# Attention heads with the values' high and low halves and ones in one stationary side of 96 columns

## What is computed

```python
def _L0_ffn_ref(x, Wq, Wk, Wv, Wo, w_ln1, w_ln2, Wr, Wg, Wu, Wd):
    xn = _rmsnorm(x, w_ln1)
    q, k, v = ...                      # 16 heads of 32 features
    attn = einsum('bqhd,bkhd->bhqk', q, k) / sqrt(32)
    attn = softmax(where(causal, attn, -inf))
    h = einsum('bhqk,bkhd->bqhd', attn, v)
    x = x + h @ Wo.T
    return x + moe(_rmsnorm(x, w_ln2))  # 8 experts, the best 2 per token
```

## Time and profile before

| | us |
|---|---|
| three executions | 1804.84, 1806.59, 1807.99 |
| median | 1806.59 |
| the profiled execution, its own time | 1806.42 |
| its span, first to last instruction | 1804.7 |
| TensorE busy | 1674.0 (93%) |
| its weight loads | 1422.9 (79%) |
| VectorE busy | 1106.8 (61%) |
| ScalarE busy | 981.3 (54%) |
| GpSimd busy | 510.0 (28%) |

### The profile page before, as it was taken

One profiled execution on the slowest core, in us unless ns is written; L12 is line 12 of the kernel. 1 busy time (PEld: TensorE's weight loads), 2 busy tenths in 40 slices (PEclk: granted clock), 3 DMA queues, 4 the chain that ended last, 5 costly groups with the idle time before them and its releaser, 6 DMA issues.

```text
span 1804.7 us, 26788 instructions
## 1 busy us (share of the span) xinstructions
PE 1674.0 (93%) x9270; PEld 1422.9 (79%) x9270; DVE 1106.8 (61%) x2076; ACT 981.3 (54%) x1713; POOL 510.0 (28%) x648
## 2 busy tenths in 40 slices
PE   3978899999989999999989999999999999999996
PEld 3666688877777777878777778898989898989895
DVE  6887732247776666676644745666666666665652
ACT  6465553335666655656553224565656656565652
POOL 3254220101212111313112022343434334343432
PEclk9989999999999999999999999999999999999998
DMA  6365558897687554875447556676767676767771
GB/s 233 94 187 185 184 168 248 231 280 256 196 266 193 174 166 114 241 199 160 147 143 181 193 199 210 227 245 231 243 227 251 228 258 225 255 226 246 233 237 24
DMA packets 119222, 370.17 MB, mean 205 GB/s; under 512 B 30175, under 2 KB 30175, under 8 KB 105378
## 3 DMA queue, kind: packets, MB, share of 16 engines
q1 hardware_dynamic: 98850, 329.36, 54.0%
q0 software_dynamic: 15696, 31.21, 9.5%
q10 hardware_dynamic: 4592, 8.52, 1.3%
HBM read 289.47 MB, written 85.72 MB: 208 GB/s over the span
## 4 chain that ended last, share of the span: by engine, by line
PE 61%; DVE 6%; ACT 5%; issue 3%; DMA 2%; SPq 1%; POOL 1%; ACTq 0%; DVEq 0%; POOLq 0%
PE bank L53 17%; PE bank L54 17%; PE bank L55 17%; PE bank L2290 2%; PE bank L2321 1%; PE bank L2318 1%; DVE hd_a L2072 1%; PE bank L2320 1%; PE bank L2276 1%; PE bank L2835 1%; ACT hd_relu L1919 1%; DVE ex_w_lo L2732 1%; DVE hd_p_lo L2139 1%; DVE hd_masked L2132 1%; ACT hd_a_hi L1940 1%
## 5 line engine op out<-in xcount | busy, mean ns | idle before, releaser
L2732 DVE TENSOR_TENSOR ex_w_lo<-ex_stage,ex_w_hi 128x1024 fp32r<-128x1024 f32 x207 | 248.7, 1237 | 166.9 <-ACT ex_w_hi L2642 162.3
L1841 POOL TENSOR_SCALAR_AFFINE_SELECT hd_p_full<-hd_p_full 128x128 f32<-128x128 f32 (+1 forms) x192 | 90.3, 478 | 433.2 <-ACT hd_p_full L1970 431.2
L2568 POOL TENSOR_TENSOR ex_a_lo<-ex_a,ex_a_hi 128x256 fp32r<-128x256 f32 x128 | 92.4, 745 | 288.4 <-ACT ex_a_hi L2664 288.2
L53 PE MATMUL bank<-ex_x_hi_a,ex_w_hi 128*128 128x256 f32 x512 | 145.0, 283 | 0.5 <-issue 0.5
L53 PE MATMUL bank<-ex_x_hi_b,ex_w_hi 128*128 128x256 f32 x512 | 144.7, 283 | 0.0
L55 PE MATMUL bank<-ex_x_hi_b,ex_w_lo 128*128 128x256 f32 x512 | 144.2, 282 | 0.0
L54 PE MATMUL bank<-ex_x_lo_b,ex_w_hi 128*128 128x256 f32 x512 | 144.2, 282 | 0.0
L55 PE MATMUL bank<-ex_x_hi_a,ex_w_lo 128*128 128x256 f32 x512 | 144.2, 282 | 0.0
L54 PE MATMUL bank<-ex_x_lo_a,ex_w_hi 128*128 128x256 f32 x512 | 144.0, 281 | 0.0
L2639 ACT ACTIVATE ex_w_hi<-ex_stage 128x1024 fp32r<-128x1024 f32 x134 | 133.7, 1048 | 0.1
L1970 ACT ACTIVATE hd_p_full<-bank 128x512 f32<-128x512 f32 (+1 forms) x192 | 93.3, 520 | 65.9 <-PE bank L2290 56.4
(11 more groups left out here) (318 smaller groups left out, 4884.6 us busy)
## 6 DMA issues: line engine op xcount, KB each, us to landing
ex_stage<-in_w_moe SPq DMA_DIRECT2D x69, 1536.0 KB, 7.7
first_w<-in_w_moe SPq DMA_DIRECT2D x23, 1536.0 KB, 6.8
hd_up<-scratch_up_halves SPq DMA_DIRECT2D x48, 512.0 KB, 6.4
hd_down<-scratch_down_halves SPq DMA_DIRECT2D x48, 512.0 KB, 6.0
st_qk<-scratch_qk SPq DMA_DIRECT2D x64, 256.0 KB, 4.2
st_qk<-scratch_qk SPq DMA_DIRECT2D x128, 64.0 KB, 3.7
scratch_up_halves<-hd_up SPq DMA_DIRECT2D x16, 512.0 KB, 3.3
scratch_down_halves<-hd_down SPq DMA_DIRECT2D x16, 512.0 KB, 3.8
```

The source lines that it names most:

```text
L53: pe.matmul(out, lhsT=w_hi, rhs=x_hi, start=first, stop=False)
L1841: pool.affine_select(out=p_full[:, i % 2, at:at + blocks * P], in_=p_full[:, i % 2, at:at + blocks * P], compare_op=ALU.is_ge, fill=0.0, b ...
L2568: pool.tensor_tensor(a_lo[:, chunk.par, m, :], a[:, m, :], a_hi[:, chunk.par, m, :].bitcast(F32), ALU.subtract).then_inc(wide_lo_ready, 1)
L2732: return dve.tensor_tensor(dst, src, hi.bitcast(F32), ALU.subtract)
```

## The change

The stationary side of a key block becomes one tile of 96 columns per head: 32 columns of high values, 32 of low values, 32 ones (`v_sides`; `v_hi`, `v_lo` and `v_one` are views of it). One matmul with `p_hi` and one with `p_lo` per key block go through it, so a head takes eight matmuls instead of twelve, and the bank then holds, for one head alone, 32 rows of high products, 32 rows of low products and 32 rows of denominators. (The product of the low halves is now part of the sum.)

Each head opens the bank anew. ScalarE copies the low rows to `o_sum` and takes Ln of the denominators after every head (`log_sums`); VectorE adds the bank's high rows to `o_sum` after every head (`add_halves`); Exp and the multiplication remain one per pair, the latter from `o_sum`. TensorE waits, ahead of a head, until both engines are through with the head before it. The split of the values takes one instruction per engine and pair instead of two. The zero fills are gone. In the diff:

```diff
--- before.py
+++ after.py
@@ -1439,8 +1439,7 @@
     STEPS = N + LAG + 2
     FIRST_PROJ = HEADS + LAG + 1
 
-    V_HI_COLS, V_HI_STEP, V_HI_TILE = 7 * HD, 4 * HD, 3 * HD
-    V_LO_COLS, V_LO_STEP, V_LO_TILE = 3 * HD, 2 * HD, HD
+    V_ROWS = 3 * HD
 
     S_PARTS = (((3, 0),), ((2, 0), (0, 3 * P)), ((1, 0),))
     T_PARTS = (((0, 0),), ((3, 0), (1, P)), ((2, 0),))
@@ -1565,8 +1564,10 @@
             hits = route.hits(lent)
         buffers.lend(buffers.OVER_VALUES)
         v_raw = sb("v_raw", [P, 2, TT, PAIR])
-        v_hi = sb("v_hi", [P, V_SLOTS, TT, V_HI_COLS], F32R)
-        v_lo = sb("v_lo", [P, V_SLOTS, TT, V_LO_COLS], F32R)
+        v_sides = sb("v_sides", [P, V_SLOTS, TT, 2, V_ROWS], F32R)
+        v_hi, v_lo, v_one = (v_sides[:, :, :, :, n * HD:(n + 1) * HD] for n in range(3))
+        o_sum = sb("o_sum", [PAIR, S])
+        sb("spare", [P, 2 * S])
         with ExitStack() as same:
             p_full, o, relu, a = (same.enter_context(nc.sbuf_tensor("hd_" + n, shape, F32)) for n, shape in (
                 ("p_full", [P, 2, PT_COLS]), ("o", [P, O_SLOTS, S]), ("relu", [P, DEEP, S]), ("a", [P, DEEP, S])))
@@ -1629,6 +1630,9 @@
         p_hi_ready = sem("p_hi_ready")
         p_lo_ready = sem("p_lo_ready")
         heads_done = sem("heads_done")
+        small_taken = sem("small_taken")
+        halves_added = sem("halves_added")
+        logs_ready = sem("logs_ready")
         rec_ready = sem("rec_ready")
         o_ready = sem("o_ready")
         o_hi_ready = sem("o_hi_ready")
@@ -1665,7 +1669,7 @@
         first_w_in = sem("first_w_in")
         first_rows = sem("first_rows")
 
-        CONSTS = 6
+        CONSTS = 3
         S_BANK, T_BANK = psum[0:2], psum[2:4]
         o_bank, misc_bank = psum[4], psum[7]
 
@@ -1806,12 +1810,9 @@
 
         @block.gpsimd
         def _(pool):
-            pool.memset(v_hi[:, :, :, :].bitcast(F32), 0.0).then_inc(consts_ready, 1)
-            pool.memset(v_lo[:, :, :, :].bitcast(F32), 0.0).then_inc(consts_ready, 1)
-            pool.wait_ge(consts_ready, 2)
-            for place in range(2):
-                at = 2 * HD + place * V_HI_STEP
-                pool.memset(v_hi[:, :, :, at:at + HD].bitcast(F32), 1.0).then_inc(consts_ready, 1)
+            for n in range(V_SLOTS):
+                i = pool.memset(v_one[:, n].bitcast(F32), 1.0)
+            i.then_inc(consts_ready, 1)
             pool.iota(prefer[:, :], [[-1, E]], base=E, channel_multiplier=0,
                       allow_small_or_imprecise_dtypes=True).then_inc(consts_ready, 1)
             pool.memset(minus_half[:, :], -0.5).then_inc(consts_ready, 1)
@@ -1974,23 +1975,25 @@
                 act.wait_ge(cut_ready, 3 * i + 3)
                 act.activation(p_hi[:, i % 2, :], p_full[:, i % 2, :], ACT.Copy).then_inc(p_hi_ready, 1)
 
+            def log_sums(h):
+                p, place = divmod(h, 2)
+                act.wait_ge(heads_done, h + 1)
+                if p and place == 0:
+                    act.wait_ge(o_ready, p)
+                own = slice(place * HD, (place + 1) * HD)
+                act.activation(o_sum[own, :], o_bank[HD:2 * HD, :], ACT.Copy).then_inc(small_taken, 1)
+                act.activation(sums_rec[own, :], o_bank[2 * HD:3 * HD, :], ACT.Ln).then_inc(logs_ready, 1)
+
             def inverse_sums(p):
-                act.wait_ge(heads_done, 2 * p + 2)
-                if p:
-                    act.wait_ge(o_ready, p)
-                act.activation(sums_rec[:, :], o_bank[PAIR:2 * PAIR, :], ACT.Ln).then_inc(rec_ready, 1)
-                act.wait_ge(rec_ready, 2 * p + 1)
+                act.wait_ge(logs_ready, 2 * p + 2)
                 act.activation(sums_rec[:, :], sums_rec[:, :], ACT.Exp, scale=-1.0).then_inc(rec_ready, 1)
 
             def high_v(p):
-                if p == 0:
-                    act.wait_ge(consts_ready, CONSTS)
                 act.wait_ge(v_in[p % 2], p // 2 * 16 + 16)
                 if p >= V_SLOTS:
                     act.wait_ge(heads_done, 2 * (p - V_SLOTS) + 2)
-                for place in range(2):
-                    act.activation(v_hi[:, p % V_SLOTS, :, place * V_HI_STEP:place * V_HI_STEP + HD],
-                                   v_raw[:, p % 2, :, place * HD:(place + 1) * HD], ACT.Copy).then_inc(v_hi_ready, 1)
+                act.activation(v_hi[:, p % V_SLOTS], v_raw[:, p % 2].rearrange("p t (u n) -> p t u n", n=HD),
+                               ACT.Copy).then_inc(v_hi_ready, 1)
 
             def high_o(p):
                 b, half, c = pair_cols(p)
@@ -2022,8 +2025,10 @@
                 for k in ks[:1]:
                     begin(k)
                     finish(k)
-                if 1 <= i <= N and i % 2 == 0:
-                    inverse_sums(i // 2 - 1)
+                if 1 <= i <= N:
+                    log_sums(i - 1)
+                    if i % 2 == 0:
+                        inverse_sums(i // 2 - 1)
                 if 0 <= i < N:
                     exps(i, 2)
                     high_p(i)
@@ -2139,14 +2144,20 @@
                 dve.tensor_tensor(p_lo[:, i % 2, :], p_full[:, i % 2, :], p_hi[:, i % 2, :].bitcast(F32),
                                   ALU.subtract).then_inc(p_lo_ready, 1)
 
+            def add_halves(h):
+                own = slice(h % 2 * HD, (h % 2 + 1) * HD)
+                dve.wait_ge(small_taken, h + 1)
+                dve.tensor_tensor(o_sum[own, :], o_bank[0:HD, :], o_sum[own, :], ALU.add).then_inc(halves_added, 1)
+
             def output(p):
                 b, half, c = pair_cols(p)
                 q = b * HC + c
                 own = slice(half * PAIR, (half + 1) * PAIR)
-                dve.wait_ge(rec_ready, 2 * p + 2)
+                dve.wait_ge(halves_added, 2 * p + 2)
+                dve.wait_ge(rec_ready, p + 1)
                 if half == 0 and q >= O_SLOTS:
                     dve.wait_ge(sum_done, sums_before[proj_at[(q - O_SLOTS) // HC]] + TT)
-                dve.tensor_tensor(o[own, q % O_SLOTS, :], o_bank[0:PAIR, :], sums_rec[:, :],
+                dve.tensor_tensor(o[own, q % O_SLOTS, :], o_sum[:, :], sums_rec[:, :],
                                   ALU.mult).then_inc(o_ready, 1)
 
             def low_o(p):
@@ -2157,13 +2168,9 @@
                                   o_hi[:, q % O_SLOTS, :].bitcast(F32), ALU.subtract).then_inc(o_lo_ready, 1)
 
             def low_v(p):
-                dve.wait_ge(v_hi_ready, 2 * p + 2)
-                for place in range(2):
-                    i = dve.tensor_tensor(v_lo[:, p % V_SLOTS, :, place * V_LO_STEP:place * V_LO_STEP + HD],
-                                          v_raw[:, p % 2, :, place * HD:(place + 1) * HD],
-                                          v_hi[:, p % V_SLOTS, :, place * V_HI_STEP:place * V_HI_STEP + HD].bitcast(F32),
-                                          ALU.subtract)
-                i.then_inc(v_lo_ready, 1)
+                dve.wait_ge(v_hi_ready, p + 1)
+                dve.tensor_tensor(v_lo[:, p % V_SLOTS], v_raw[:, p % 2].rearrange("p t (u n) -> p t u n", n=HD),
+                                  v_hi[:, p % V_SLOTS].bitcast(F32), ALU.subtract).then_inc(v_lo_ready, 1)
 
             def per_tile(x):
                 return x.unsqueeze(2).to_broadcast([P, TT, E])
@@ -2224,6 +2231,8 @@
                     finish(k)
                 if s < N:
                     maxima(s, 2)
+                if 1 <= i <= N:
+                    add_halves(i - 1)
                 if s % 2 == 1 and 0 <= (s - 7) // 2 < N // 2:
                     output((s - 7) // 2)
                 for k in ks[1:]:
@@ -2308,18 +2317,15 @@
                     pe.wait_ge(a_full, ups_before[TWO_UPS])
                 if place == 0:
                     pe.wait_ge(v_lo_ready, p + 1)
-                    if p:
-                        pe.wait_ge(o_ready, p)
+                if h:
+                    pe.wait_ge(logs_ready, h)
+                    pe.wait_ge(halves_added, h)
                 for kt in range(TT):
                     at = slice(T_AT[kt], T_AT[kt] + (TT - kt) * P)
-                    queries = slice(kt * P, S)
-                    high = v_hi[:, p % V_SLOTS, kt, place * V_HI_TILE:place * V_HI_TILE + 2 * PAIR]
-                    low = v_lo[:, p % V_SLOTS, kt, place * V_LO_TILE:place * V_LO_TILE + PAIR]
-                    pe.matmul(o_bank[:, queries], lhsT=high, rhs=p_hi[:, h % 2, at], start=(place == 0 and kt == 0),
-                              stop=False)
-                    pe.matmul(o_bank[0:PAIR, queries], lhsT=low, rhs=p_hi[:, h % 2, at], start=False, stop=False)
-                    last = pe.matmul(o_bank[:, queries], lhsT=high, rhs=p_lo[:, h % 2, at], start=False,
-                                     stop=(place == 1 and kt == TT - 1))
+                    sides = v_sides[:, p % V_SLOTS, kt, place, :]
+                    out = o_bank[0:V_ROWS, kt * P:S]
+                    pe.matmul(out, lhsT=sides, rhs=p_hi[:, h % 2, at], start=(kt == 0), stop=False)
```

(1 more changed line is left out.)

## The result

Four executions of each kernel on one chip: before 1805.7 us (1804.4 to 1808.0), after 1831.6 us (1830.7 to 1833.1), ratio 1.014 [1.013, 1.015]. The change makes the kernel slower by 26 us. The forecast was 1812, the range reached to 1832.

What follows compares the result with a forecast made beforehand. TensorE bounds some intervals between heads, ScalarE's work ahead of the third exponent others. Terms −7.5 + 4.4 + 0.7 + 3 + 4.9 = +5.5 us gave 1812 us; the forecast's own range was 1803 to 1820, with rivals 1785 to 1832.

Steps and rivals of the forecast that it cites:

- rival B, VectorE's queue: VectorE's addition per head delays the work queued behind it: +20 to +27 us, 1830; chance 0.16.
- The passes: TensorE's value matmuls, eight instead of twelve a head: 0.58 us less a head, 37 us if all of it counted.
- two pieces, the second a sum: Head intervals with two feed-forward pieces, ending in a down sum, TensorE full: −0.58 us each for 13, −7.5.
- what I had left over: The 3 remaining intervals between heads, waiting elsewhere: 0.
- one piece, begun by a sum, even: 11 one-piece intervals after even heads, becoming ScalarE's: 6.2 to 6.4 us against 5.94, +0.4 each, +4.4.
- the same, odd: 8 one-piece intervals begun by a sum, after odd heads: 6.98 us against 7.00, so 0.
- one piece, begun by an up piece: One-piece intervals where ScalarE's new work adds whole: 7 even +0.1 each, +0.7; 6 odd +0.5 each, +3.
- two pieces, the second an up piece: 15 intervals waiting on ScalarE's relu: 7 begun by a sum 0; 8 begun by an up piece +0.8 even, +0.5 odd, +4.9.
- The saving is spent on the copy: One-piece intervals begun by a sum, after odd heads: TensorE's saving goes to ScalarE's copy, change 0.
- A: Rival: TensorE pays all that it saves: −18 us, 1788, at its end −37, 1769; chance 0.27.
- C: Rival: 96-column passes take 1.5 times today's pitch, so eight last as long as twelve: +24 us, 1830; chance 0.05.

Runs made afterwards that it cites:

- kernel 7: The changed kernel with VectorE's addition and the waits for it left out (high rows missing from the output): 1828.4 us.
- kernel 1: The kernel before without the low values' product (L2320), so eight passes a head and nothing else changed: 1792.6 us, ratio 0.993 to before.
- Kernels 5 and 6: The changed kernel with discarded 512-column matmuls where TensorE waits: 5 ahead of the scores of 13 heads, 1829.0 us; 6 with 15 heads more, 1832.7 us.
- kernel 9: The changed kernel with four discarded matmuls in each of the 20 heads where TensorE had the most slack: 1828.2 us.
- kernels 3, 9 and 12: 12: kernel 3 with the third exponent ahead of Ln after even heads, between Ln and Exp after odd ones: 1794.6 us; kernel 3 and kernel 9 have their own lines.
- kernel 3: The changed kernel with the copy of the low rows moved from ScalarE to VectorE, just before its addition: 1803.0 us, ratio 0.999 to before.
- kernel 2: The changed kernel with four discarded matmuls more per head, so that TensorE has twelve again: 1844.8 us, ratio 1.022 to before.

## Why the prediction was right or wrong

**The number**: the sign is right, the size is not. +5.5 us was forecast, with 1803 to 1820 as the forecast's own range, and +26 measured. That 1831.6 still lies below 1832 is luck: the range reached that far for the sake of rival B, VectorE's queue, and kernel 7 refutes B.

**The passes**: right. 1.20 us instead of 1.82 for a head, −0.62 where I took −0.58.

**The intervals**: mostly right. In the 48 that are at full clock in both traces, the sum of the differences is +4.8 us; +5.5 was forecast for all 63. By term, each as mean of the intervals at full clock against the forecast:

1. two pieces, the second a sum (15 with what I had left over): −0.37 (forecast −0.58 for 13), so 5.5 us instead of 7.5. Some give −0.62, others nothing; 652.67 is one of these, 8.73 us for 8.76 with 8.44 busy: TensorE was full there and now waits.
2. one piece, begun by a sum, even: +0.59, median +0.47 (forecast +0.4). 5.94 became 6.43 where 6.2 to 6.4 was written.
3. the same, odd: +0.06 over 7 (forecast 0).
4. one piece, begun by an up piece: even +0.07 over 5 (+0.1); odd, the one pair at full clock, +0.22 (+0.5). The other five of these six are at the lower clock, and hold +7.6 us where 2.5 were forecast.
5. two pieces, the second an up piece: begun by a sum −0.04 even and +0.42 odd (0); begun by an up piece +0.69 even (+0.8) and +0.66 odd (+0.5).

One price in these was off: I took 0.53 us from the copy to Ln, and in even heads from Ln to the exponent, the pitch of two instructions that don't depend on each other. It is 0.61 (662.80 to 663.41), as for those that do. The even twin, 706.58, shows the chain of term 2 whole:

```profile
708.05 0.59 ACT L1984 ACTIVATE hd_o_sum<-bank 32x512 f32<-32x512 f32 x1 [1.56 <-PE bank L2328]
708.67 0.59 ACT L1985 ACTIVATE hd_sums_rec<-bank 32x512 f32<-32x512 f32 x1
709.28 0.38 ACT L1971 ACTIVATE hd_p_full<-bank 128x256 f32<-128x256 f32 x1
```

From the head's first matmul to the copy it takes 1.47 us (I had 1.12 + 0.32), to Ln 0.62 and to the exponent 0.61 (0.53 each), and the next head starts 3.73 behind the exponent, at 713.01, as I had it: 6.43. TensorE idles there 0.39 us for VectorE's maxima, at 708.82, and hardly any for the exponent (0.11), where the forecast had it wait for the exponent alone.

**What failed** is a step that has no term in the sum. Where a saving doesn't reach the end of an interval, I priced TensorE's added idle time at nothing: "The saving is spent on the copy", 0. The other 15 intervals, at the lower clock in one trace or the other, hold +26.4 of the +31.3, the clock's part and what the queues cost in them together. The odd interval from 666.77 shows it; its counterpart is 678.27, with 0.68 in the clock column and 10.75 us instead of 7.81. TensorE in it, in order of time:

```profile
679.54 0.33 PE L2299 MATMUL bank<-st_qk 97*128 97x256 f32 x1
681.62 1.01 PE L2309 MATMUL bank<-ident,hd_row_max 128*4 128x128 f32 x4 [1.75 <-DVE hd_row_max L2137]
...
684.36 0.63 PE L53 MATMUL bank<-st_x_hi,hd_up 128*128 128x512 f32 x1
...
685.64 0.63 PE L53 MATMUL bank<-st_x_hi,hd_up 128*128 128x512 f32 x1
...
687.34 0.63 PE L54 MATMUL bank<-st_x_lo,hd_up 128*128 128x512 f32 x1
...
688.90 0.28 PE L2285 MATMUL bank<-st_qk 96*128 96x256 f32 x1
```

It idled 1.75 us ahead of the transposes at 681.62, and from there three 512-column matmuls take 1.28 us (684.36 to 685.64) until 688.20; at the full clock they take 0.69 (665.52 to 666.21).

What the lower clock costs can be read where nothing was changed. The rest of the kernel behind the heads took 841.2 to 842.2 us in the three traces in which TensorE had no lower clock there, and 844.8 to 846.7 in the seven with 10.2 us of it; the line through all 14 traces gives 0.43 us for each us. Among the 64 executions of before on record, time against mean clock gives less, 0.31. The first price also explains most of after's −5.2 there (none against 10.2 us, 4.4). At these prices 51.2 − 6.8 = 44.4 us in the phase are 14 to 19 us; the other 12 to 17 of the 31.3 are queues. It is an estimate, since neither price was read in this phase of after. It isn't one execution's accident: the mean clock of the four executions of after is 0.971 to 0.975, that of the 64 of before 0.977 to 0.987. Between the averages of these lie 40 us at the lower clock over the whole kernel, by the same prices 12 to 17 of the 26 us.

I had read the clock column of before (1.00 in nearly all of the earlier trace rows) and taken it as given. Yet the forecast's own terms said that TensorE would idle more: 546 − 64 x 0.58 = 509 us busy in 594, 86% instead of the 93% of the earlier trace rows. I drew nothing from that.

**The rivals.** A needed 5.94 to fall; it rose to 6.43. B: kernel 7. C: loads of 164 ns and 1.20 us a head. The 164 ns lie on the line through the loads of 64 and 128 columns. What the Trainium skill says in TensorE: Matmul & The Clock Gate, Weight-path perf modes (a fast load at 128 columns unless the type is FP32) shows in none of these loads. The Trainium skill's advice to improve the engine with the highest occupancy (Perfetto Trace Analysis, Identifying the Most-Contended Engine) would have given A, and these runs don't bear it out: TensorE got 252 matmuls less in the phase, and the kernel lost 26 us; kernel 1 shows that even with nothing added in return, 12 of 37 us arrive.

**What stays open**: which idle times lower the clock. Kernels 5 and 6 filled some and changed it little, kernel 9 filled others and changed it more. That kernels 3, 9 and 12 have a higher clock because TensorE waits less at those places is argued, not shown. So is the split between clock and queues in kernel 3's 29 us. Each kernel has one profiled execution, so a few us at the lower clock between two kernels mean nothing.

## What to carry to other kernels

An engine at 93% busy is not the bound wherever its idle times end behind another engine's instruction: there, work put into that other engine's queue ahead of the instruction waited for is paid in full, and which queue it stands in counts more than its amount. Here 43 us of additions on VectorE cost 3 us, and 38 us of copies on ScalarE 29; one reordering (the exponent ahead of Ln) was worth 8. And TensorE's idle time has a price: when a change shortens its work without shortening the interval, forecast the clock too, from an unchanged stage of the same traces.

## What the hardware showed beyond this

The granted clock doesn't follow the sum of TensorE's idle time: 60.5 us of it in the phase went with 44.4 us at the lower clock in kernel 6, 65.4 with 20.5 in kernel 2. Nor does it take one long gap: in before, where TensorE's longest was 2.5 us, it fell twice in the phase, each time behind gaps of 1.4 to 1.5 us. VectorE's addition from rows 0 to 31 of the bank starts, in the odd head above, at 663.42, beside ScalarE's Ln of rows 64 to 95 of the same bank (663.41), and takes 0.68 us, the mean of its group, as did the 64 rows before. The copy, Ln and Exp on ScalarE start 0.61 to 0.62 us apart, whether they depend on each other or not, with 0.59 of work in copy and Ln, while two exponents of 128x512 in a row start 0.48 apart with 0.58 of work.
